# Two groups of transposes change their place in the attention phase of a graph and mixture-of-experts kernel

## The reference

```python
Xp = jnp.einsum('bnd,hdk->bhnk', X, Wp) + bp[None, :, None, :]
Xc = jnp.einsum('bhnk,hjk->bhnj', Xp, C)
attn = jnp.tanh(A[:, None] * jnp.einsum('bhnj,bhmj->bhnm', Xc, Xp))
Xh = jnp.einsum('bhnm,bhmk->bhnk', attn, Xp)
out = jnp.moveaxis(Xh, 1, 2).reshape(X.shape[0], X.shape[1], -1)
return jax.nn.relu(out)
...
shared = jax.nn.silu(xf @ sw1) * (xf @ sw3) @ sw2
```

## Time and profile before

| what | us |
|---|---|
| median of 3 runs | 2244.68 |
| lowest and highest | 2244.51, 2255.48 |
| the profiled execution | 2249.72 |
| its span | 2247.9 |

### The profile page before, as it was taken

How to read it: one execution, slowest core, us unless ns; L and a number is a source line. 1 busy time by engine, 2 the same in 40 slices (tenths; PEclk the granted TensorE clock), 3 DMA queues, 4 the chain that set the end, 5 groups by cost and what they waited for, 6 DMA issues and landing times. The chain is left out here.

```text
span 2247.9 us, 38345 instructions
## 1 busy us (share of the span) xinstructions
PE 2065.9 (92%) x12128; PEld 1509.9 (67%) x12128; DVE 1537.5 (68%) x3332; ACT 1249.5 (56%) x1870; POOL 1065.9 (47%) x1266
## 2 busy tenths in 40 slices
PE   7999999947999999958999999998999789999986
PEld 6988888846888888843444444444444478878853
DVE  6777777744666666645777778767776557767759
ACT  4444444404666666646676666755655357767630
POOL 3455555541333333326455545556432447777740
PEclk9999999968999999988999999978776899999998
DMA  7444445124555555542232112222210055655559
GB/s 286 147 169 167 170 170 179 44 103 149 180 179 179 177 178 180 179 158 96 73 118 80 60 60 78 82 91 70 71 66 32 6 174 182 189 166 191 184 195 355
DMA packets 138147, 315.40 MB, mean 140 GB/s; under 512 B 36990, under 2 KB 67808, under 8 KB 133952
## 3 DMA queue, kind: packets, MB, share of 16 engines
q1 hardware_dynamic: 106560, 271.77, 36.1%
q0 software_dynamic: 31488, 42.39, 5.5%
HBM read 206.67 MB, written 151.56 MB: 159 GB/s over the span
## 5 line engine op out<-in xcount | busy, mean ns | idle before, releaser
L1699 ACT ACTIVATE c_att<-c_att 128x1024 f32<-128x1024 f32 x256 | 270.5, 1057 | 214.0 <-DVE c_att L1901 212.1
L1901 DVE TENSOR_TENSOR c_att<-c_p_s,adj 128x1024 f32<-128x1024 f32 x256 | 302.4, 1217 | 104.5 <-PE c_p_o L1421 87.9
L2228 POOL DMA_INDIRECT moe_y<-d_y,d_goal x256 | 257.4, 1006 | 115.9 <-ACT d_y L2193 51.2
L995 POOL DMA_INDIRECT moe_y<-b_y,b_goal x144 | 156.7, 1088 | 325.5 <-DVE b_y L1047 291.7
L1408 PEld LDWEIGHTS c_p_s<-c_xcth,c_xpth 32*128 32x128 f32 x512 | 51.5, 199 | 224.6 <-issue 132.7
L154 PE MATMUL b_p_y<-b_w2h,b_hh 128*128 128x256 f32 x576 | 168.9, 293 | 6.4 <-DVE b_hl L160 3.5
L476 POOL DMA_INDIRECT moe_in<-a_xn,a_rows x128 | 141.6, 1107 | 57.6 <-issue 29.2
L1408 PE MATMUL c_p_s<-c_xcth,c_xpth 32*128 32x512 f32 x512 | 140.2, 546 | 29.4 <-DVE c_att L1901 28.5
L1421 PE MATMUL c_p_o<-c_att,c_xp 128*32 128x512 f32 x1024 | 161.5, 708 | 2.2 <-ACT c_att L1699 1.2
L160 DVE TENSOR_TENSOR b_hl<-b_ht,b_hh 128x512 fp32r<-128x512 f32 (+1 forms) x160 | 101.6, 639 | 88.7 <-ACT b_ht L1153 88.6
L155 PE MATMUL b_p_y<-b_w2l,b_hh 128*128 128x256 f32 x576 | 160.6, 279 | 0.0
(11 more groups left out here) (271 smaller groups left out, 6143.0 us busy)
## 6 DMA issues: line engine op xcount, KB each, us to landing
b_w<-in_moe_w SPq DMA_DIRECT2D x80, 512.0 KB, 6.1
moe_in<-b_zeros SPq DMA_DIRECT2D x65, 520.0 KB, 10.9
d_xin<-moe_in SPq DMA_DIRECT2D x64, 520.0 KB, 3.6
adj<-in_adj SPq DMA_DIRECT2D x32, 1024.0 KB, 5.4
b_xin<-moe_in SPq DMA_DIRECT2D x32, 520.0 KB, 5.9
c_g<-moe_y SPq DMA_DIRECT2D x32, 512.0 KB
moe_y<-c_zeros SPq DMA_DIRECT2D x32, 512.0 KB, 6.8
d_w<-in_moe_w SPq DMA_DIRECT2D x64, 256.0 KB
```

Source lines behind the costliest of these rows:

```text
L995: pool.indirect_dma_start(out=m["moe0_y"], out_offset=bass.IndirectOffsetOnAxis(ap=goal[:, h, t:t + 1], axis=0), in_=y[:, h, t, :], in_off ...
L1699: act.activation(part, part, ACT.Tanh).then_inc(att_ready, 1)
L1901: dve.tensor_tensor(att[:, u % 2, 2 * c:2 * c + 2, :], p_s[:, 2 * c:2 * c + 2, :], adj[:, h, u % T, :].unsqueeze(1).broadcast_to([P, 2, N] ...
L2228: pool.indirect_dma_start(out=m["moe1_y"], out_offset=bass.IndirectOffsetOnAxis(ap=goal[:, h, t:t + 1], axis=0), in_=y[:, h, t, :], in_off ...
```

## The change

In the graphs whose predecessor has no shared expert in this phase (`light`, b = 9 to 15) the turn back of the second half moves from unit 5 to unit 7, on TensorE, and its copy by ScalarE from unit 6 to the end of unit 7. In the graphs 10 to 14 the turn of the first half of the normed rows moves from unit 2 to the end of unit 1. Graph 15 is the last and has neither of the moved steps.

```diff
@@ TensorE, graph @@
+                light = post and not going_up
...
                         pe.wait_ge(xn_ready, b + 2)
                         if going_down:
                             pe.wait_ge(x4_ready, TB * (b - 2) + 1)
-                        else:
+                        elif not late:
                             pe.wait_ge(xct_lo, GRP * b + GRP)
-                        turn(xn, 0, z, tr_done)
+                        if going_down or not late:
+                            turn(xn, 0, z, tr_done)
...
+                    if u == 7 and light and not last:
+                        pe.wait_ge(xct_lo, GRP * (b + 1) + 1)
+                        turn_back(xpf[:, 1], 2, xp_done)
...
-                    if u == 5 and not last:
+                    if u == 5 and not last and not light:
                         pe.wait_ge(xct_lo, GRP * (b + 1) + 1)
                         turn_back(xpf[:, 1], 2, xp_done)
+                    if u == 1 and not last and late and not going_down:
+                        pe.wait_ge(xn_ready, b + 2)
+                        pe.wait_ge(xct_lo, GRP * b + GRP)
+                        turn(xn, 0, z, tr_done)
@@ ScalarE, graph @@
+                light = post and b - 1 >= OWN
...
-                    if u == 6 and not last:
+                    if u == 6 and not last and not light:
                         evac_tokens(b + 1, 1 - h, 1)
...
+                    if u == 7 and light and not last:
+                        evac_tokens(b + 1, 1 - h, 1)
```

## The result

The changed kernel takes 2243.70 us as the median of 16 runs (2236.49 to 2247.55), the kernel before 2250.93 us as the median of 16 (2244.51 to 2262.20). The ratio is 0.9965, with a 95% interval of 0.995 to 0.998: 4.5 to 11.3 us faster, 7.9 in the middle. A second comparison, on another chip, gave 0.995 (0.9930 to 0.9971). The forecast was 12.8 us less than before, and 2232.

The account below looks back on a forecast made before the run. The prediction took TensorE, falling to half clock in the light graphs, as the bound. Lifts worth 15.4 us, coming in five of six graphs, made 12.8; from a median of 2244.7 that gave 2231.9, said as 2232, range 2222 to 2251.

Parts of the forecast that it names:

- The bound: Light graphs, unit 6 to unit 1: TensorE is busy to the last at half clock, which lengthens the stretches between marks.
- Leaving unit 5 brings nothing: Unit 5: the 0.66 us turn lay in idle time, so the wait becomes 1.8 us and the clock falls as now.
- The lift behind the turn in unit 7: Unit 7: turn touching values raises the clock in about five in six graphs; stretches take 20.4 us, gaining 15.4 x 5/6 = 12.8.
- no fall comes there: Gap at unit 1: sign expected in the profile after, with half the turn of normed rows standing in that gap.
- The second part: Half the normed-row turn moved from unit 2 into unit 1's gap: alone worth at most 5.5 us, at worst losing 0.2 a graph.
- the first part: Turn back moved from unit 5 to unit 7: costs 1.11 us six times, 6.7 us, but may lift the clock there.
- the sum: Whole kernel: 12.8 us gained, one miss cancelling (1.1 lost, 1.1 won); 2244.7 - 12.8 = 2231.9, said as 2232.
- the term of 12.8 us: Light graphs: 15.4 us of gains between the marks into graphs 10 to 15, times 5/6 for lifts that miss.
- Rival 1: Unit 7: no lift comes and the turn only costs, 6.7 us less up to 5.5 back; 2248 as middle; chance 0.12.
- Rival 2: Unit 7: the lift comes in only some graphs, 4.4 to 7.7 us less than now; 2239 as middle; chance 0.17.
- Rival 3: Units 5 and 6: the deeper gap keeps the clock down until unit 3, 14.6 us more; 2259; chance 0.10.
- Rival 4: Unit 6: the clock is kept right through it as well, 27 us gained in all; 2217; chance 0.06.

Follow-up runs that it names:

- turn_only: Changed kernel without the move to unit 7, keeping the half turn of normed rows at the end of unit 1: 0.9995 of the kernel before.
- back_extra1: Changed kernel with all eight normed-row transposes back in unit 2, plus four extra transposes at the end of unit 1: 1.0056 of the kernel before.
- back_only: Changed kernel without the turn of normed rows in unit 1, keeping the turn back in unit 7: 1.0069 of the kernel before.
- the fillings: Unneeded transposes or products added in TensorE's waits, to the changed kernel or (unit 5 only) the kernel before: 0.9831 to 0.9937 of the kernel before.

## Why the prediction was right in kind and wrong in size

*The bound* (clock of 0.5 between unit 6 and unit 1) was right: any work that holds it at 1.00 gains, up to 1.7%.

*Leaving unit 5 brings nothing*: right as to place; the wait became 1.75 us, and the clock fell in unit 6 in 17 of 18 graphs, after 14 of 18 before. But nothing was the wrong price for that gap as a place to put things: 1.1 us of transposes in it are worth 1%.

*The lift behind the turn in unit 7*: right, and in 17 of 17 where I had said five in six. The stretches between the marks took 13.1 us less in the mean of three profiles each, for a forecast of 12.8. That the two are so near is luck: the stretches took 19 to 22 us each and not 20.4, for the lift came more often than I had allowed and won more, and falls in the gap at unit 1 and 2, ten in three profiles and seven of them for 10 us, took part of it back. I had named that fall as what would make me wrong, and written "no fall comes there".

*The second part*: its own size, 0 to 5.5 us, was right by the ratio of turn_only, but its role was wrong. I had it fill the gap in unit 1. back_extra1 (1.0056) shows that filling that gap does not save the first part; without the freed unit 2 it stays slower than the kernel before. Alone the first part costs 15.5 us, with the second it gains 8 to 11, and I had priced the two as a sum.

*The step that failed* is the sum. It set a gain read from one execution against another set of runs: "against the median it is 2244.7 - 12.8". The median of three runs was 6.2 us below the median of 16, so the forecast time came out low by as much, 2238.1 by the later median. The profiled execution's own 2249.7, which I corrected downward by 5.0, was the better base. The rest, 5.6 us to the measured 2243.7, is the term of 12.8 us, which the timed runs put at 7.9 (4.5 to 11.3), and the second comparison at 11.2 (6.5 to 15.7). The profiles, three of each kernel, say 13.1 in the mean. Why the 16 runs show less than the profiles isn't settled, but the clock points to the choice of executions: the one profiled of the 16 had a mean clock of 0.947, the highest among them, and their median was 0.943. So the usual one spent more time at half clock; whether lifts were missing or more falls came behind them, no trace tells. In the second comparison the median of the runs was 0.947, as in the profiles, and the gain was 11.2 us. Executions of these two kernels differ by 11 and 18 us.

*The rivals.* Rival 1, the turn only costs, is what the first part does alone: 15.5 us, more than twice the 6.7 that I gave it. In its profile the second fall of a graph lasts 10 us where that of graph 12 before lasted 3.4, and a graph takes 51.2 us instead of 47.9. The Trainium skill ("TensorE: Matmul & The Clock Gate", Part 4, PE-mode transpose) says that the full clock does not engage for transposes. The runs here decide otherwise: with eight transposes in the gap of unit 5 the clock fell in unit 6 in none of 12 graphs, as with plain products (none of six). That the kernel would change sides on the place of a clock switch, within about 2 us of the turn, I hadn't seen: I treated the wander of the falls as luck per graph, while the profiles suggest that it hangs on the length of the graph itself. Rival 2, a lift in only some graphs, had 4.4 to 7.7 us, which is near what the 16 runs gave, but in the three profiles no lift was missing. Rival 3, a deeper gap that keeps the clock down until unit 3, did not come: back_only rises in between and falls twice. Rival 4, the clock kept through unit 6, is what the fillings bring about by other means, at 26 to 38 us, where I had 27.

## What to carry to other kernels

Where the trace shows PE at half clock and busy to the last, look for the wait ahead of the fall and put work into it, even work without use; that gave 0.6% alone and 1.4% with this change, which by itself gave 0.4 to 0.5%. Two moves that act on the clock can't be priced one by one, as +15.5 and -1 us against -8 to -11 together show: run each alone and both together. Take the base of a forecast from as many executions as there are, read a gain in the clock from more than one profile, and compare the mean clock of the profiled execution with that of the timed runs before taking it for the usual one.

## What the runs showed of the hardware

The switches of the clock can settle into step with the graph: in the profile of back_only the five periods from `c_member` to `c_member` are 51.4, 51.4, 51.2, 50.9 and 51.1 us, each with a fall about unit 6 and one about unit 2, while the same work takes 42.7 to 48.6 us in the three profiles of the changed kernel. With the same turn and values in unit 7 the clock rose in 17 of 17 cases where they began 6.2 to 7.6 us behind the fall, and in none of 9 where they began 8.3 to 8.5 us behind it; why isn't shown. Transposes held the clock as well as products did: with eight of them in a gap of 1.8 us a stretch of 74 us went by at full clock, where in the light graphs of the changed kernel none was over 35 us.
